# A two-block image network on one core: relus to VectorE, squares to ScalarE, two value buffers, shorter routing products, and zeros ahead of each sample

## The reference

```python
# block 1: similarity mixer, then a mixture of 16 experts (top 2 by softmax)
xn  = x * rsqrt(sum(x*x))
sim = relu(xn @ xn.T) ** 2
x1  = x + sim @ (x @ W)
x2  = x1 + sum over the 2 best experts of  p_e * (silu(n(x1) w1_e) * (n(x1) w2_e)) w3_e
# block 2: deformable 3x3 convolution, then a feed-forward for the better half of the tokens
om     = conv3x3(n(x2));  offsets, mask = om[:18], sigmoid(om[18:])
value  = bilinear samples of the padded map at 9 shifted places, times mask   # 9 * 64 per token
x3     = x2 + value @ dcn_weight
weight = n(x3) @ wr + br;  out = x3 + (token chosen by weight) * weight * ffn(n(x3))
```

## Time and profile before

| | |
|---|---|
| median of 3 runs | 4409.18 us |
| profiled execution | 4427.31 us, its span 4425.5 us |
| busy share: PE, DVE, ACT, POOL | 66%, 55%, 40%, 66% |
| mean granted TensorE clock | 0.704 |
| gathers of corners (L548), 1800 | 2029.3 us busy, mean 1127 ns; first at 720.5 us |
| DVE squares (L951), 496 | 479.7 us busy |
| ACT relus (L1515), 800; ACT squares (L1544), 304 | 643.2 us; 259.5 us |
| PE idle before sample transposes (L1724) | 522.3 us |
| last image's first gather | 3962.6 us |

### The profile page before, as it was taken

How to read it: one execution, slowest core, us unless ns; L and a number is a source line. 1 busy time by engine, 2 the same in 40 slices (tenths; PEclk the granted TensorE clock), 3 DMA queues, 4 the chain that set the end, 5 groups by cost and what they waited for, 6 DMA issues and landing times.

```text
span 4425.5 us, 51603 instructions
## 1 busy us (share of the span) xinstructions
PE 2910.2 (66%) x17810; PEld 1891.5 (43%) x17810; DVE 2435.6 (55%) x3747; ACT 1761.2 (40%) x2959; POOL 2925.6 (66%) x2608
## 2 busy tenths in 40 slices
PE   5969687586757786777777676788681357146432
PEld 2434534452446345633465345633460146135321
DVE  6354454744675456655665466655654245345775
ACT  5656466245523562355425552365231112122210
POOL 0040074777777776777767777777777777776770
PEclk8979798678856895678667886589665556555555
DMA  5000214321533132423342144313351325243446
GB/s 123 8 15 9 39 24 102 100 77 50 127 96 96 39 106 82 131 54 97 85 116 77 51 110 111 110 33 107 87 133 47 104 88 131 62 127 91 121 111 120
DMA packets 540746, 375.76 MB, mean 85 GB/s; under 512 B 465872, under 2 KB 470736, under 8 KB 540496
## 3 DMA queue, kind: packets, MB, share of 16 engines
q0 software_dynamic: 110848, 257.07, 20.1%
q1 hardware_dynamic: 429648, 115.40, 12.5%
HBM read 308.79 MB, written 89.41 MB: 90 GB/s over the span
## 4 chain that ended last, share of the span: by engine, by line
POOL 43%; PE 23%; issue 13%; DVE 11%; ACT 4%; DMA 3%; DVEq 2%; SPq 1%; ACTq 0%; POOLq 0%
POOL G L548 28%; PE PS L1689 22%; POOL shared L562 9%; POOL slot_rows L554 6%; DVE G L623 2%; DMA G<-corner_table,index 2%; DVE G L629 1%; DMA out<-experts_w 1%; DVEq L625 1%; DVE small L972 1%; DVE value L631 1%; PE PS L1724 1%; DVE st L590 1%; ACT small L1551 0%; DVE smallc L590 0%
## 5 line engine op out<-in xcount | busy, mean ns | idle before, releaser
L548 POOL DMA_INDIRECT G<-corner_table,index x1800 | 2029.3, 1127 | 681.6 <-issue 537.0
L623 DVE TENSOR_TENSOR G<-G,corner_w 128x768 f32<-128x768 f32 x600 | 541.5, 953 | 678.2 <-DMA G<-corner_table,index 678.1
L1515 ACT ACTIVATE work<-PS 128x768 f32<-128x768 f32 (+2 forms) x800 | 643.2, 822 | 541.9 <-PE PS L1689 277.8
L1689 PE MATMUL PS<-xn 128*128 128x400 f16 (+3 forms) x3200 | 647.9, 346 | 236.0 <-ACT work L1515 229.8
L951 DVE TENSOR_TENSOR work<-work 128x768 f32<-128x768 f32 (+2 forms) x496 | 479.7, 973 | 457.0 <-PE PS L1689 415.3
L554 POOL DMA_INDIRECT slot_rows<-split_a,slot x400 | 485.1, 1213 | 335.1 <-DVE slot L1046 213.5
L562 POOL DMA_INDIRECT shared<-slot_results,slot x400 | 410.1, 1025 | 349.5 <-DMA slot_results<-shared 227.8
L1689 PE MATMUL PS<-work,xm 128*64 128x400 f32 (+3 forms) x3200 | 638.0, 517 | 0.0
L1689 PEld LDWEIGHTS PS<-xn 128*128 128x128 f16 (+1 forms) x3200 | 289.8, 101 | 666.4 <-ACT work L1515 389.2
L1724 PE MATMUL PS<-ident,value 128*128 128x128 f32 x800 | 181.8, 370 | 522.3 <-DVE xq L636 275.5
L1423 ACT ACTIVATE val_cm<-PS 128x512 f32<-128x512 f32 x200 | 119.1, 596 | 694.5 <-PE PS L1724 694.3
(11 more groups left out here) (266 smaller groups left out, 3591.7 us busy)
## 6 DMA issues: line engine op xcount, KB each, us to landing
G<-corner_table,index POOLq DMA_INDIRECT x1800
corner_table<-rows_scratch SPq DMA_DIRECT2D x32, 784.0 KB
shared<-slot_rows SPq DMA_DIRECT2D x32, 512.0 KB, 7.6
slot_results<-shared SPq DMA_DIRECT2D x32, 512.0 KB
corner_table<-G SPq DMA_DIRECT2D x8, 841.0 KB, 10.5
slot_rows<-split_a,slot POOLq DMA_INDIRECT x400
shared<-slot_results,slot POOLq DMA_INDIRECT x400
experts_w<-x_scratch SPq DMA_DIRECT2D x8, 784.0 KB, 6.2
```

Source lines behind the costliest of these rows:

```text
L548: GP.indirect_dma_start(G[0:rows, n % 2, tap * 4 * C:(tap + 1) * 4 * C], None, tables[b % 2], bass.IndirectOffsetOnAxis(ap=index[0:rows, c ...
L623: V.tensor_tensor(g, g, bc(w, 2, C), ALU.mult)
L1515: A.activation(relu[0:rows, u % 2, :, 0:n], PS[u % 2][0:rows, :, 0:n], ACT.Relu).then_inc(s["relu_done"], 1)
L1689: return P.matmul(o, a, b, start=start, stop=stop, skip_group_check=True)
```

## The change

1. In the mixer DVE now forms the relu of its five steps from PSUM, and ACT all eight squares. `relu_done`, `sq_act`, `sq_dve` become `relu_act`, `relu_dve`, `squared`.
2. `value` becomes two buffers; its writer waits for the transposes of the tile two before. The column form goes, and with it `ident2` (two loads), `dcn_cm`, the third ACT copy and the fourth stage of a sample.
3. The weighing of turn 0 (tile 23) stands in the mixer's second half, ahead of the y sums, in units 0 to 7.
4. Routing in the feed-forward of the turns: 28 products with two columns each, which DVE adds up with a reduce.
5. `sample` waits for `conv_added`, then, in turns and in the tail, multiplies six times zeros by zeros into `D0` (400 columns), and then waits for `valued`.
6. `sel` and `eq16` lie in memory that other tensors have; no instruction follows from it.

```diff
-MIX_SAMPLE, MIX_EVAC, MIX_ADD, MIX_WEIGH = (0, 2, 4, 6), (1, 3, 5), 7, (2, 3, 4, 6, 7)
+MIX_SAMPLE, MIX_EVAC, MIX_ADD, MIX_WEIGH = (0, 2, 4), (1, 3), 7, (2, 3, 4, 6, 7)
-SLOTS, TAIL_SLOTS = 19, 8
+SLOTS, TAIL_SLOTS, FILL = 19, 8, 6
 ...
 # DVE, weigh
-                    if piece == 4 and b * T + t > 0:
-                        dve.wait_ge(s["val_tr"], 2 * (b * T + t))
+                    if piece == 4 and b * T + t > 1:
+                        dve.wait_ge(s["val_tr"], 2 * (b * T + t - 1))
 ...
 # DVE, mixer
-                                dve.wait_ge(s["relu_done"], g + u + 1)
-                                free = squares_taken(hn, g + u)
-                                if free > 0:
-                                    dve.wait_ge(s["mixed"], free)
-                                V.tensor_tensor(sq[0:rows, u % 4, :, 0:n], relu[...], relu[...], ALU.mult).then_inc(s["sq_dve"], 1)
+                                dve.wait_ge(s["sim_done"], g + u + 1)
+                                if g + u > 1:
+                                    dve.wait_ge(s["squared"], g + u - 1)
+                                V.tensor_scalar(relu[0:rows, u % 2, :, 0:n], PS[u % 2][0:rows, :, 0:n], 0.0, None,
+                                                ALU.max).then_inc(s["relu_dve"], 1)
                             beside_mixer(k, j, u)
 ...
+                    if half:
+                        turn_weighing(k, 0)
                     for m in range(2):
                         dve.wait_ge(s["y_done"], k * 4 + half * 2 + m + 1)
 ...
 # ACT, mixer
+            def square_step(s_no, half, jh, u):
+                hn, rows, n = s_no // SPH, tile_rows(jh * JB + u // 2), IWS[half]
+                (wait for relu_dve or relu_act of step u, and for mixed of step u - 4)
+                A.activation(sq[0:rows, u % 4, :, 0:n], relu[0:rows, u % 2, :, 0:n], ACT.Square).then_inc(s["squared"], 1)
 ...
+                            if u + 1 in ACT_STEPS and u + 1 < steps(jh):
+                                if u:
+                                    act.wait_ge(s["squared"], g + u)
+                                relu_step(g + u + 1, half, jh, u + 1)
+                            if u == SPB - 1:
+                                act.wait_ge(s["squared"], g + u)
+                                relu_step(g + SPB, half, jh + 1, 0)
+                            square_step(g + u, half, jh, u)
 ...
 # PE, sample
-                    pe.wait_ge(s["valued"], n)
                     if n > 1:
                         pe.wait_ge(s["conv_added"], n - 1)
+                    for _ in range(fill):
+                        mm(D0[:, 0:max(IWS)], zero16[:, 0:128], zero16[:, :])
+                    pe.wait_ge(s["valued"], n)
 ...
 # PE, ffn_down
-                        for w in (wrh, wrl):
-                            ins = mm(Y1[0:RP, 448 + t:449 + t], xf[:, t * RP:(t + 1) * RP], w[:, 0:1], w is wrh, w is wrl)
+                        ins = mm(Y1[0:RP, 448 + 2 * t:450 + 2 * t], xf[:, t * RP:(t + 1) * RP], wr2[:, :])
```

More of the change, by code:

```diff
@@ L192, in metaformer_kernel @@
         stage3 = work
-        value = sb("value", [TP, TAPS * C])
+        values = sb("values", [TP, 2, TAPS * C])
         val_cm = sb("val_cm", [128, 5 * TP])
-        dcn_cm = sb("dcn_cm", [128, TP])
         w_all = sb("w_all", [RP, B, RT])
@@ L630, in weigh @@
                     else:
[L631 removed]
+                        V.tensor_tensor(values[:, q, :].rearrange("p (n c) -> p n c", n=TAPS), g[:, :, 0, :], g[:, :, 1, :],
                                         ALU.add).then_inc(s["valued"], 1)
@@ L937, in idle_mixer, with turn_weighing @@
                         beside_mixer(k, j, u)
+            def turn_weighing(k, r):
+                b, t = turn_weigh(k, r)
+                if turn_holds(k, b):
+                    for piece in range(5):
+                        weigh(b, t, piece)
             def mixer(k):
@@ L1101, in turn @@
                         ln_center("a", xm, x1, 0, q)
[L1102 to L1105, removed]
+                if k >= B or r:
+                    turn_weighing(k, r)
                 b, t = turn_sample(k, r)
@@ L1426, in sample_evac @@
                     A.activation(val_cm[:, 4 * TP:5 * TP], D0[:, 0:TP], ACT.Copy).then_inc(s["val_ready"], 1)
-                if stage == 2 and not token_form(b, t):
-                    act.wait_ge(s["conv_done"], column_tiles(b, t))
-                    A.activation(dcn_cm[:, :], D0[:, 128:128 + TP], ACT.Copy).then_inc(s["conv_ready"], 1)
             def geo_table(q):
@@ L1502, in beside_mixer @@
                     ffn_prepare(k - 4, j, u)
-                for stage in range(3):
+                for stage in range(2):
                     if valid(k - 3) and j in LATE_SAMPLE and MIX_EVAC[stage] == u:
@@ L1663, in _ @@
             for t in range(T):
-                for n in range(3):
+                for n in range(2):
                     sample_evac(LAST, t, n)
@@ L1712, in stacks, with sample @@
                     pe.wait_ge(s["n_cm"], (k + 1) * 2 * NCH)
-            def sample(b, t, stage):
+            def sample(b, t, stage, fill=0):
                 n = b * T + t + 1
+                value = values[:, (n - 1) % 2, :]
                 if stage == 0:
-                    pe.wait_ge(s["valued"], n)
                     if n > 1:
                         pe.wait_ge(s["conv_added"], n - 1)
+                    for _ in range(fill):
+                        mm(D0[:, 0:max(IWS)], zero16[:, 0:128], zero16[:, :])
+                    pe.wait_ge(s["valued"], n)
                     for i in range(4):
@@ L1808, in sims, with wait_relu @@
                 ins.then_inc(s["sim_done"], 1)
+            def wait_relu(hn, jh, u):
+                if u in ACT_STEPS:
+                    pe.wait_ge(s["relu_act"], relus_act(hn, jh, u))
+                else:
+                    pe.wait_ge(s["relu_dve"], relus_dve(hn, jh, u))
             def mix(half, hn, jh, u):
@@ L1826, in beside_mixer @@
                     ffn_prepare(k - 4, j, v)
-                for stage in range(4):
+                for stage in range(3):
                     if valid(k - 3) and j in LATE_SAMPLE and MIX_SAMPLE[stage] == v:
@@ L1969, in turn @@
                 if turn_holds(k, b):
-                    for stage in range(4):
-                        sample(b, t, stage)
+                    for stage in range(3):
+                        sample(b, t, stage, FILL)
                 if k < B and r == A_TURN:
@@ L2061, in _ @@
             for t in range(T):
-                for n in range(4):
-                    sample(LAST, t, n)
+                for n in range(3):
+                    sample(LAST, t, n, FILL)
                 if t == 2:
```

88 lines of the change are left out of this document (31 added, 57 removed).

## The result

The changed kernel takes 4395.31 us (median of 19 runs, 4385.19 to 4407.80); the kernel before, beside it, 4420.54 (19 runs, 4400.55 to 4440.85). The ratio is 0.9947, 95% interval 0.9933 to 0.9961: faster by 0.53%, some 23 us, where I had forecast 38.

What follows compares the result with a forecast made beforehand. POOL's gather instructions plus pauses bound about 720 to 3962 us, PE the mixers before, DVE and PE the tail. Terms +7 - 45 + 10 - 16 + 4 + 5 - 3 = -38 us gave 4371 from 4409.18; range 4280 to 4440.

Steps and rivals of the forecast that it cites:

- The zeros: Six zero products ahead of samples: partly hidden in PE's waits, nearly even; +4 us in turns, +5 in the tail.
- The clock: Rival, chance 0.20: zeros lift PE's clock in turns and tail, POOL's pauses go; about 4300 us.
- The stretch of 39 us at 0.50: PE ahead of the gate's counts (1710 to 1749 us), busy at low clock; taken to occur in four images.
- POOL and the squares: Units 3 to 7: without DVE's SBUF-reading squares POOL's gathers and scatters run shorter; -45 us (bounds -80 and 0).
- The +10: Units 3 to 7: DVE's relus stand behind weighing and gather waits; +2 us each, +10 (bounds -25 and +40).
- The signs named: If right, in a mixer's first part: POOL's scatters near 1.1 us instead of 1315 ns, gathers of results near 0.95.
- an estimate of 100 us: By the SBUF exclusion rule, POOL waits half a square on average: about 20 us per mixer, 100 in all; not adopted.
- the rows' 45: POOL's gain over five mixers as taken from profile rows, 9 us each where POOL leads: -45 us.
- The lead-in: Ahead of the first gather: relus on DVE lengthen PE's loop by 1 to 2%; +7 us (bounds -10 and +15).
- The moved weighing: Tile 23 weighed while DVE waits for y: 4 us in four images, -16 (bounds -20 and +10).
- The condition given with the step: Tile 23's gathers must have landed; if late by x, turn 0 is late by x less 5 us.
- The rest: Token form and second value buffer taken as 0; shorter routing, 28 products instead of 56, -3 us.

Runs made afterwards that it cites:

- add_first: Changed kernel, zeros kept, but in the tail DVE adds the previous tile's sample before weighing the next tile; 4387.6 us, ratio 0.9937 to the kernel before.
- no_zeros: Changed kernel without any products of zeros, in turns or tail; 4377.1 us, ratio 0.9901 to the kernel before.
- others_only: Changed kernel with the mixers' earlier relu/square assignment, tile 23 weighed in the first turn, no products of zeros; 4402.8 us, ratio 0.9973 to the kernel before.
- the fastest kernel: Changed kernel with earlier relu/square assignment in the first three mixers, no zeros, tail add before weighing from tile 9; 4362.7 us, 0.9880 of the kernel before.

## Why the prediction was wrong

**The zeros** were the mis-sized term: +9 forecast, +18 to +20 measured (good to some 10; of the +5 for the tail alone, 9 in the profiles). The step that failed: "Where PE waits for the value they are hidden (the transposes at 4166.67 had waited 7.24 us)". The row there names what ended that wait, and it is `DVE xq L636`, the add of the sample before, not `value L631`. The zeros stand behind the wait for that add. One view of the kernel before says it for all samples, PE's waits ahead of the instructions that read the value (us, times; images 0 on):
```profile
its engine sat idle before it (us, times) until:
  DVE xq L636: 266.6, 52
  DVE value L631: 244.4, 12
```
Four waits in five ended on the add, and half of the time waited. In the changed kernel, ahead of the zeros:
```profile
L1683 PE MATMUL PS<-zero x968: 326/537/541, 771.8 to 4325.2; 128*128 128x400 f16 x192, 128*128 128x384 f16 x2
its engine sat idle before it (us, times) until:
  DVE xq L628: 232.9, 48
```
(948 of the 968 are the samples'.) 48 samples' waits now stand ahead of their zeros, so that in these places, where I took them as hidden, they are paid. What they take (2.0 us each time) was right; what they give back I had taken as nearly even, and it was 1.3 us in the tile above and nothing in others. Which samples make up the 18 to 20 us was not traced.

**The clock** as a rival had the wrong price: it wanted POOL's pauses gone, and these grew from 48.6 to 60.1 us. The stretch of 39 us at 0.50, taken for four images, was there in two: units 6 and 7 of the kernel before ran it at 0.73 and 0.81. The clock rose in the tail, to 0.81 in the 3.9 us behind the zeros of the tile above:
```profile
4125.20:4127.20 2.00, 1.93 (x6) 0.97 (x7) 1.81 (x3) 0.00 (x0) 1.37 (x1) 0.50 0.20 66
4127.20:4131.10 3.90, 2.73 (x17) 2.04 (x15) 1.65 (x2) 1.48 (x3) 2.99 (x4) 0.81 0.22 67
```
and in add_first, where the zeros lie 2.7 us ahead of the sample, it did not (the sample's stretch):
```profile
4135.30:4140.40 5.10, 3.92 (x16) 3.20 (x16) 3.43 (x4) 1.71 (x3) 3.75 (x3) 0.50 0.17 42
```
The Trainium skill (TensorE: Matmul & The Clock Gate, "What's actually happening") has activity release a throttle that is on by default; these rows agree, and show that in this tile the release is worth 1.3 us where 2 are spent on it. Nor did it always come: in 7 of the last image's 25 samples in the changed kernel the clock stayed at 0.50 right behind the zeros, and the sample took 4.9 us as without them. One of the seven (its zeros start at 4062.10):
```profile
4064.10:4069.00 4.90, 3.84 (x17) 3.12 (x15) 1.57 (x1) 1.64 (x3) 3.68 (x5) 0.50 1.27 231
```

**POOL and the squares**: right in kind. Taken out of the changed kernel, the split is worth 28 us with the lead-in in it, taken out of no_zeros 44 (each good to some 10); my three terms for it, +7, -45 and +10, make -28. The +10, for mixers that wait for DVE's relus, doesn't show: from the first similarity to the last, the mixers of units 3 to 7 take 216 to 218 us after and 222 to 226 before, with the whole change in. The signs named, scatters near 1.1 us and result gathers near 0.95, came at 1201 and 980 ns; with the split of before and the rest of the change but no move and no zeros (others_only) the means of the five units stay at 1248 and 1051, against 1261 and 1050 before. The Trainium skill's rule (SBUF — State Buffer, "SBUF: two separate sides") had given an estimate of 100 us; POOL is 66 us less busy, between that and the rows' 45, and 11.5 us of it went into longer waits for values.

**The lead-in**: +7 forecast, 11 measured. The bare mixers were as worked out (1.5 and 2.2 us longer); the third was taken like them and cost 10.

**The moved weighing**: -16 forecast, -23 out of the changed kernel, and nothing with the old split. That the first two lie near each other is luck: the forecast took 4 us off each pause at tile 6, and these are 10.6 us in images 2 to 4 with the move and without. The waits that it does remove, at tile 0, are not in the kernel before; they come with the faster POOL. The condition given with the step (gathers late by x, turn 0 late by x less 5 us) is what the 8.90 us show. It should have tied this term to POOL's: split and move together bring 32 us (others_only to no_zeros), while their terms, +7, -45, +10 and -16, add up to 44 and the two runs without one of them to 51. Each of those two runs loses what only both together give.

**The rest**: -3 forecast, -12 measured, because I looked at PE's products alone; what the token form's fewer hand-overs per tile give was not isolated.

So, from -38: zeros +11, split and move +12, the rest -9, which makes -24; each of these is good to some 10 us. That the two profiled executions differ by 35 us, close to the forecast, is chance: the first lay 7 us above its median, the second 3 below.

## What to carry to other kernels

Before filling a wait, read what ends it and whether the filler is queued ahead of that wait or behind it: if behind, that wait does not hide it. An engine that runs the gathers can be sped up from another engine's choice of operands, here by taking 496 squares of SBUF tiles off DVE; do that only in stages where the gathers run. A step that is moved to an earlier place is worth what its inputs' arrival allows, so it is priced together with the edit that brings them forward, not added to it. And a clock read in one unit is no effect of an edit until the same stretch has been read in the kernel without the edit, in every unit.

## What the runs showed of the hardware that was not expected

Six products of 400 columns ahead of a sample raised the granted clock at most for what followed directly: in the tile shown, the sample's eight small products took 1.00 us right behind them and 1.81 us after a pause of 2.7 us, as without them; in 7 of 25 samples not even right behind them. Ahead of the gate's counts the same program, without any zeros, got 0.76 in one unit and 0.55 in the next. And the mean granted clock says nothing of the time here: 0.757 with zeros at 4395 us, 0.71 without at 4377, 0.705 in the fastest kernel.
